# A softmax attention kernel: its row sums spread by one selection matmul, and the reciprocal taken of the spread sums

## What is computed

```python
x = x + attention(_ln_c(x))       # 8 heads of 16 channels
t = x.reshape(768, 128)
t = t + ffn(_ln_t(t))
# attention, per head:
att = q @ k.T / sqrt(16) + time_bias + particle_bias, masked by time
att = softmax(att, axis=-1)
y   = concat over heads(att @ v) @ Wo
# ffn: 8 experts (128 -> 512 -> 128), all of them, for each of the 2 gate weights of a token
h   = gelu((x * p_i) @ W1 + b1);  out += h @ W2 + sum(b2)
```

## Time and profile before

| | |
|---|---|
| median of 3 runs | 2684.5 us |
| the profiled execution, its own time | 2693.18 us |
| its span, first to last instruction | 2691.2 us |
| mean granted TensorE clock, share of full speed | 0.897 |
| PE matmul busy | 2328.3 us (87%) |
| DVE busy | 1373.4 us (51%) |
| ACT busy | 1661.6 us (62%) |
| POOL busy | 1050.5 us (39%) |

### The profile page before, as it was taken

The page is one execution under the profiler, slowest core; times in us unless marked ns, Lnnn a source line. Parts: engine busy times, 40 slices in busy tenths (PEclk is TensorE's granted clock), DMA queues, the critical chain, the costliest instruction groups (busy, mean ns, idle before and its releaser), DMA issues.

```text
span 2691.2 us, 54396 instructions
## 1 busy us (share of the span) xinstructions
PE 2328.3 (87%) x17443; PEld 2071.1 (77%) x17443; DVE 1373.4 (51%) x3267; ACT 1661.6 (62%) x2760; POOL 1050.5 (39%) x1048
## 2 busy tenths in 40 slices
PE   1659988898898989988898998989889898998889
PEld 0448887787878878887787888778787887888778
DVE  2324473554537544573554547455463654447354
ACT  3227567566665657666566765757666566756757
POOL 1104343343434434352443434434342443434347
PEclk7668898999989989998999899989998998899899
DMA  3413022030212203022130302203021120302200
GB/s 47 75 38 45 8 30 26 14 45 7 34 19 33 26 9 47 10 27 26 21 38 7 42 11 32 27 10 45 10 28 26 28 30 8 49 7 30 26 10 7
DMA packets 70219, 71.22 MB, mean 26 GB/s; under 512 B 20462, under 2 KB 55242, under 8 KB 69962
## 3 DMA queue, kind: packets, MB, share of 16 engines
q1 hardware_dynamic: 69746, 67.64, 18.3%
q10 hardware_dynamic: 216, 0.08, 0.0%
HBM read 11.22 MB, written 6.29 MB: 7 GB/s over the span
## 4 chain that ended last, share of the span: by engine, by line
PE 64%; issue 12%; DVE 11%; ACT 9%; SPq 2%; POOL 1%; DMA 0%; DVEq 0%; ACTq 0%; POOLq 0%
PE acc L858 18%; PE wide L784 9%; PE narrow L798 7%; PE zps L847 7%; PE zps L848 5%; PE zps L849 5%; ACT z L490 5%; PE wide L769 5%; DVE maxes L633 3%; DVE h L691 2%; PE wide L812 2%; PE wide L819 2%; PE wide L805 1%; ACT L490 1%; ACT h L519 1%
## 5 line engine op out<-in xcount | busy, mean ns | idle before, releaser
L431 POOL TENSOR_TENSOR hsum<-h 128x384 f32<-128x384 f32 x1024 | 1028.8, 1008 | 1553.6 <-ACT h L519 1533.3
L691 DVE TENSOR_TENSOR h<-zps,ratio_b 128x384 f32<-128x384 f32 x1024 | 561.0, 552 | 928.2 <-PE zps L849 925.9
L518 ACT ACTIVATE h<-zps,b_col 128x384 f32<-128x384 f32 x1024 | 593.5, 580 | 678.4 <-DVE h L691 659.2
L858 PE MATMUL acc<-w,hsum 128*128 128x128 f32 x6144 | 872.3, 279 | 1.5 <-DVE outt L700 1.2
L858 PEld LDWEIGHTS acc<-w,hsum 128*128 128x128 f32 x6144 | 857.1, 196 | 2.2 <-POOL hsum L431 1.7
L519 ACT ACTIVATE h<-h,b_col 128x384 f32<-128x384 f32 x1024 | 620.5, 606 | 0.0
L847 PE MATMUL zps<-x_hi,w_lo 128*128 128x384 f32 x1024 | 428.6, 419 | 88.2 <-DVE x_lo L670 47.9
L633 DVE TENSOR_REDUCE maxes<-wide 128x1 f32<-128x128 f32 (+5 forms) x768 | 437.3, 616 | 87.5 <-PE wide L769 83.8
L784 PE MATMUL wide<-stack 128*128 128x256 f32 (+3 forms) x1280 | 348.9, 432 | 108.2 <-ACT z L490 82.9
L784 PEld LDWEIGHTS wide<-stack 128*128 128x128 f32 x1280 | 264.1, 284 | 187.4 <-ACT z L490 159.0
L490 ACT ACTIVATE z<-wide 128x896 f32<-128x896 f32 (+2 forms) x384 | 343.5, 916 | 63.8 <-PE wide L784 54.9
(11 more groups left out here) (89 smaller groups left out, 1282.8 us busy)
## 6 DMA issues: line engine op xcount, KB each, us to landing
stack<-halves SPq DMA_DIRECT2D x384, 96.0 KB, 3.0
stack<-halves SPq DMA_DIRECT2D x384, 24.0 KB, 2.6
x_in<-in_x SPq DMA_DIRECT2D x136, 48.0 KB, 2.4
out_dram<-outt SPq DMA_DIRECT2D x256, 24.0 KB, 1.6
w<-in_L_ffn_W SPq DMA_DIRECT2D x8, 256.0 KB, 4.3
stack<-max_rows SPq DMA_DIRECT2D x128, 3.0 KB
stack<-max_rows SPq DMA_DIRECT2D x128, 1.5 KB
stack<-z SPq DMA_DIRECT2D x6, 192.0 KB
```

The costliest lines, as they stand in the source:

```text
L431: pool.tensor_tensor(hsum[:, m % NHS, :], h0[:, m % 2, :], h1[:, m % NH1, :], ALU.add).then_inc(hsum_ready, 1)
L518: act.activation(h0[:, m % 2, :], zps[m % 2][:, 0:CT], ACT.Gelu, bias=b1_col[:, j:j + 1]).then_inc(h0_ready, 1)
L691: vec.tensor_tensor(h1[:, m % NH1, :], zps[m % 2][:, 0:CT], ratio_b[:, c * CT:(c + 1) * CT], ALU.mult).then_inc(z1_ready, 1)
L858: ins = pe.matmul(acc[:, n * P:(n + 1) * P], hsum[:, k % NHS, n * P:(n + 1) * P], w2[:, j, :], start=(j == 0 and n == 0), stop=(j == UNITS ...
```

## The change

- Steps *sums* are gone, with `recip` and its small reciprocal.
- `pick` becomes a 128x128 matrix: column c of head hh's 32 columns has a one in row 32hh+16, so it selects that head's sum. In *divide* it is the weights, and `mixed` streams through it in two matmuls of 512 and 256 columns. That gives, in one step, each head's sum repeated over its 32 rows, 128x768.
- DVE then takes the reciprocal of all 128x768 in place in PSUM, waits for its own result (`inverted`), and multiplies `mixed` with it.
- *divide* of group 0 moves to slot 31, ahead of the two *maxima* there; *divide* of group 1 to slot 46, and *project* from slot 49 to 48.
- `xn_ready` after the gate's scaling counts once per half, so the first *split* waits for three of the six products instead of all.

```diff
--- before.py
+++ after.py
@@ -63,10 +63,10 @@
     for hh in range(GH):
         plan += [(26, "scores", (0, hh, n)) for n in range(3)] + [(26, "stack", (1, hh))]
     plan += [(27, "mix", (0, 0)), (28, "mix", (0, 1))]
-    late = [(30, "sums", 0), (32, "divide", 0)] + maxima(1, (31, 31, 32, 33, 34, 36, 36, 37, 38, 39, 39, 40))
+    late = [(31, "divide", 0)] + maxima(1, (31, 31, 32, 33, 34, 36, 36, 37, 38, 39, 39, 40))
     plan += sorted(late, key=lambda step: step[0]) + [(41, "rows", 1)]
     plan += [(44, "scores", (1, n // 3, n % 3)) for n in range(12)]
-    plan += [(44, "mix", (1, 0)), (45, "mix", (1, 1)), (46, "sums", 1), (47, "divide", 1), (49, "project", 0), (50, "load", 1)]
+    plan += [(44, "mix", (1, 0)), (45, "mix", (1, 1)), (46, "divide", 1), (48, "project", 0), (50, "load", 1)]
     plan += [(50, "stats", 1), (51, "seed", 1), (51, "root", (1, 0)), (52, "root", (1, 1)), (52, "root", (1, 2)),
              (54, "scale", (1, 0)), (54, "scale", (1, 1)), (56, "turn", 1), (57, "gate", 0), (58, "weigh", 0),
              (60, "split", 0), (60, "split", 1)]
@@ -74,7 +74,7 @@
 
 
 PLAN = attention_plan()
-WIDE_STEPS = ("turn", "query", "key", "value", "maxima", "rows", "scores", "sums", "divide", "project", "split")
+WIDE_STEPS = ("turn", "query", "key", "value", "maxima", "rows", "scores", "divide", "project", "split")
 NARROW_STEPS = ("mix", "gate")
 
 WIDE = {(s, a): n for n, (s, a) in enumerate([(s, a) for _, s, a in PLAN if s in WIDE_STEPS])}
@@ -128,7 +128,7 @@
         wo_pad = sb("wo_pad", [P, GROUPS, C])
         wg = sb("wg", [P, EXPERTS])
         ident = sb("ident", [P, P])
-        pick = sb("pick", [P, GH])
+        pick = sb("pick", [P, GH, 2 * HD])
 
 
         x_in = sb("x_in", [P, TILES, C])
@@ -145,7 +145,6 @@
         kst = stack[:, HEADS * QW:].rearrange("p (h t) -> p h t", h=GH)
         z = sb("z", [P, GH, ZW])
         maxes = sb("maxes", [P, GH * TILES])
-        recip = sb("recip", [P, TILES, GH])
         max_rows = sb("max_rows", [GH * TILES, P])
         stats = act_t[:, 0:TILES * 6].rearrange("p (i s) -> p i s", s=6)
         moments = sb("moments", [P, TILES, 2])
@@ -228,6 +227,7 @@
         gate_exped = sem("gate_exped")
         split_high = sem("split_high")
         res_ready = sem("res_ready")
+        inverted = sem("inverted")
 
         z_filled = sem("z_filled")
         z1_ready = sem("z1_ready")
@@ -387,7 +387,7 @@
 
         @block.gpsimd
         def _(pool):
-            cleared = ((wo_pad[:, :, :], 0.0), (ident[:, :], 0.0), (hot_stage, 0.0), (pick[:, :], 0.0),
+            cleared = ((wo_pad[:, :, :], 0.0), (ident[:, :], 0.0), (hot_stage, 0.0), (pick[:, :, :], 0.0),
                        (twos, 2.0), (ones, 1.0), (t_hl, 0.0), (p_hl, 0.0))
             later = ((kst[32:64, :, :].bitcast(F32), 0.0), (kst[64:P, :, :].bitcast(F32), 0.0),
                      (spread[0:40, :, 0:PAD], 0.0), (val[:, :, :, HD:2 * HD], 1.0))
@@ -400,7 +400,7 @@
                 done += 1
 
 
-            hots = [(ident[:, :], 0, [[-1, P]]), (pick[:, :], -HD, [[-32, GH]])]
+            hots = [(ident[:, :], 0, [[-1, P]]), (pick[:, :, :].rearrange("p a b -> p (a b)"), -HD, [[-32, GH], [0, 2 * HD]])]
             times, parts = [[-1, TPT], [0, PARTS]], [[0, TPT], [-1, PARTS]]
             hots += [(hot_stage[0:TPT, :], 0, times), (hot_stage[32:32 + PART_N, :], 1, parts)]
             for buf, base, pattern in hots:
@@ -632,15 +632,14 @@
                     for i, at in (((0, 0), (5, P)), ((4, P), (1, 6 * P)), ((3, P), (2, 5 * P)))[part]:
                         ins = vec.tensor_reduce(maxes[:, hh * TILES + i:hh * TILES + i + 1], w[:, at:at + (i + 1) * P], AX.X, ALU.max)
                     ins.then_inc(wide_free[s], 1)
-                elif step == "sums":
-                    vec.wait_ge(wide_filled[s], filled)
-                    vec.reciprocal(recip[:, :, :], w[:, 0:TILES * GH].rearrange("p (i g) -> p i g", g=GH)).then_inc(wide_free[s], 1)
                 elif step == "divide":
                     vec.wait_ge(wide_filled[s], filled)
                     if a == 1:
 
                         for hh in range(GH):
                             vec.wait_ge(stack_loaded[hh], r.at(GROUPS * STACK_DMAS * 16, GROUPS * STACK_DMAS * 16))
+                    vec.reciprocal(w[:, 0:TOK], w[:, 0:TOK]).then_inc(inverted, 1)
+                    vec.wait_ge(inverted, r.at(GROUPS, a + 1))
                     vec.tensor_tensor(mixed_n[a][:, 0:TOK], mixed[:, :], w[:, 0:TOK], ALU.mult).then_inc(wide_free[s], 1)
                 elif step == "project":
                     vec.wait_ge(wide_filled[s], filled)
@@ -663,7 +662,8 @@
                     vec.tensor_tensor(ratio[:, :, 1], top[:, :, 1], gate_r[:, :], ALU.mult)
                     for i in range(TILES):
                         ins = vec.tensor_scalar(xn[:, i, :], xn[:, i, :], top[:, i, 0:1], None, ALU.mult)
-                    ins.then_inc(xn_ready, 1)
+                        if i % HT == HT - 1:
+                            ins.then_inc(xn_ready, 1)
                     assert chain[0] == VCHAIN
                 elif step == "split":
                     vec.wait_ge(split_high, r.at(4, 2 * a + 2))
@@ -742,7 +742,7 @@
                     if not (isinstance(free, int) and free <= 0):
                         pe.wait_ge(narrow_free, free)
                 if step == "turn":
-                    pe.wait_ge(xn_ready, r.at(5, 2 * (a + 1)))
+                    pe.wait_ge(xn_ready, r.at(6, 2 * (a + 1)))
                     for i in range(TILES):
                         ins = pe.transpose(w[:, i * P:(i + 1) * P], xn[:, i, :], ident[:, :])
                     ins.then_inc(wide_filled[s], 1)
@@ -798,20 +798,12 @@
                             ins = pe.matmul(narrow[32 * hh:32 * hh + 32, q0:width], val[:, i, g * GH + hh, :],
                                             z[:, hh, at:at + width - q0], start=(n == 0), stop=(n == len(tiles) - 1))
                     ins.then_inc(narrow_filled, 1)
-                elif step == "sums":
+                elif step == "divide":
 
                     pe.wait_ge(narrow_free, r.at(NPB, NARROW["mix", (a, 1)] + 1))
-                    for i in range(TILES):
-                        ins = pe.matmul(w[:, i * GH:(i + 1) * GH], mixed[:, i * P:(i + 1) * P], pick[:, :], start=True, stop=True)
-                    ins.then_inc(wide_filled[s], 1)
-                elif step == "divide":
-
-                    pe.wait_ge(*taken(r, "sums", a))
-                    for i in range(TILES):
-                        for hh in range(GH):
-                            ins = pe.matmul(w[32 * hh:32 * hh + 32, i * P:(i + 1) * P], recip[:, i, hh:hh + 1].broadcast_to([P, 32]),
-                                            ident[:, :], start=True, stop=True)
-                    ins.then_inc(wide_filled[s], 1)
+                    sums = pick[:, :, :].rearrange("p h d -> p (h d)")
+                    pe.matmul(w[:, 0:QCOLS], sums, mixed[:, 0:QCOLS], start=True, stop=True)
+                    pe.matmul(w[:, QCOLS:TOK], sums, mixed[:, QCOLS:TOK], start=True, stop=True).then_inc(wide_filled[s], 1)
                 elif step == "project":
                     pe.wait_ge(*taken(r, "divide", 1))
                     for i in range(TILES):
@@ -826,7 +818,7 @@
                                         start=True, stop=True)
                     ins.then_inc(narrow_filled, 1)
                 elif step == "split":
-                    pe.wait_ge(xn_ready, r.at(5, 5))
+                    pe.wait_ge(xn_ready, r.at(6, 5 + a))
                     for n in range(HT):
                         i = a * HT + n
                         pe.transpose(w[:, n * P:(n + 1) * P], xn[:, i, :], ident[:, :])
```

## The result

| | before | after |
|---|---|---|
| median | 2684.86 us (4 runs, 2684.5 to 2685.81) | 2854.35 us (4 runs, 2849.92 to 2858.97) |
| the profiled execution, own time | 2693.18 us | 2858.61 us |
| its span | 2691.2 us | 2856.8 us |
| mean granted TensorE clock | 0.897 | 0.870 |

The ratio is 1.0631, with a 95% interval of 1.0608 to 1.0654: slower by 169.5 us. The forecast was 141 us more, 2826 us, with a range of 2770 to 2880. The direction and the mechanism held; the size was 28 us short. It lies 4 us above the 2800 to 2850 that stood for the forecast case (chance 0.63), towards the case with the clock low for twice as long (0.05).

A forecast was written before the change was run, and what follows sets the result against it. It took PE as the bound (busy 87%), with DVE also full around group 0's division. Per round 4.45 + 1.0 + 2.1 + 1.45 = 9.0 us, times 15 = 135, plus 6.3 before the loop: +141, 2826 us, range 2770 to 2880.

The forecast's parts named there:

- the forecast case: Whole kernel: clock loss behind the PE waits within a few tenths of the forecast, 2800 to 2850 us, chance 0.63.
- the case with the clock low for twice as long: Behind both PE waits: a larger loss, bounded at 2.9 us each, chance 0.05.
- The reciprocal's duration: DVE in both divisions: 768 elements at 6.4 ns each plus 153 ns fixed take 5.1 us.
- Rival C: DVE in both divisions: slower reciprocal, 8.3 ns an element, 6.55 us, giving 2872 us; chance 0.09.
- E: DVE rival: part of the small reciprocals' difference is the source, 3.2 ns an element, 2.6 us, about 2703 us; chance 0.03.
- Rival D: DVE: cheap reciprocal, nearly all fixed cost, 0.95 us for 768 elements, so faster, 2660 us; chance 0.03.
- The net -1.65 us of PE per group: PE in each division: 2.94 us of sums and divide go, two selection matmuls of 1.29 us come in.
- Group 0's wait and its carry-over: Slot 31: PE stands 5.7 us for DVE before the second maxima step, and DVE ends up 4.45 us later.
- Group 1's wait and carry-over: Before the projection: PE stands 3.8 us for DVE, and the next unit starts 2.1 us later.
- The clock: Behind both PE waits the clock falls to 0.50: +1.0 us in group 0, +1.45 in group 1, bounds 0 and 2.9 each.
- Given back: Rest of the round: other edits costed at nothing, though the earlier split could give up to 5 us in all.
- In front of the loop: Attention before the loop: two divisions, each 3.15 us longer with no units to hide it, together +6.3 us.

The follow-up runs named there:

- kernel 7: Kernel before with only group 0 changed to selection matmuls and a reciprocal deferred to slot 44, group 1 as before: 2684.98 us, 0.9992.
- kernel 4: Changed kernel with matmuls nobody reads put into PE's two waits, 8 before the second maxima step and 6 before the projection: 2825.08 us, 1.0509 to the kernel before.
- kernel 5: Kernel before with the count of xn_ready per half as the only edit: 2686.77 us, 0.9993.
- kernel 9: Kernel before with the projection in slot 48 instead of 49 as the only edit: 2686.23 us, 0.9999.
- kernel 10: Kernel before with five matmuls nobody reads put into PE's wait between the split and unit 64: 2686.01 us, 0.9997.
- kernel 1: Changed kernel with a copy of the same 128x768 in place of the reciprocal in both groups: 2663.01 us, 0.9912 to the kernel before.
- kernel 3: Changed kernel with a copy in place of the reciprocal in group 1 alone: 2742.38 us, 1.0210 to the kernel before.
- kernel 6: Changed kernel with group 0's reciprocal moved to slot 44 and group 1's split in two, the first beside the second mix: 2637.77 us, 0.9816 to the kernel before.
- kernel 8: Kernel before with group 1 selected and inverted in two pieces, projection in slot 48, xn_ready per half, group 0 as before: 2651.86 us, 0.9871.

## Why the prediction was right, and where its size was off

- **The reciprocal's duration** (5.1 us): 4.97 measured. The slope, 6.4 ns an element from two small rows, measures 6.25. Rival C's rate of 8.3 and E's of 3.2 are both ruled out, and so is D's.
- **The net -1.65 us of PE per group:** the selection's matmuls are spaced as forecast, but where the saving lands matters more. In group 0 only 0.70 us of it shows even when the reciprocal is out of the way (kernel 7), so PE's matmuls were not the only limit there. The sum for the changed kernel had this right, since it went by DVE in group 0.
- **Group 0's wait and its carry-over** (5.7 and +4.45 us): the wait was 5.59. With the clock held up the stage is 36.19 - 31.30 = 4.89 us longer, against 4.45.
- **Group 1's wait and carry-over** (3.8 and +2.1): the wait was 4.01. With the clock held up, 33.64 - 30.52 = 3.12, 1.0 more than forecast. Of this, 0.6 lies in front of the division: from group 1's first mix matmul to the next unit kernel 4 takes 4.35 us and the kernel before 3.74, with the clock low for 3.0 us of it instead of 1.8. The other 0.4 I cannot assign.
- **The clock** (1.0 and 1.45): this is the term that was too small. Kernel 4 gives 1.60 in group 0 and 2.15 in group 1 (of which 2.44 in the projection, less 0.3 elsewhere in the stage). I took the 1.44 us of one short idle stretch as the price of any; behind the longer waits the clock stayed down for 3 us in some rounds and for 6 in others, and through the whole projection in all of them. I had that as the bound (2.9) and not as the value.
- **Given back:** I had costed the rest of the round at nothing. Behind the gate the changed kernel is 1.51 us a round faster than before. In the kernel before, the clock falls there behind two waits of PE in each round; in most rounds of the changed kernel the query comes 3.1 instead of 4.7 us after turn 0, at full speed. All kernels with group 1's new form but kernel 4 have it. In the kernel before, neither the `xn_ready` edit (kernel 5) nor the projection's slot (kernel 9, 0.64 of it at most) nor work put into PE's wait behind the split (kernel 10) brings it.
- **What the rounds show of it:** the query comes 4.7 us after turn 0 in all 14 rounds of the kernel before, and 3.1 in 11 of the changed kernel's; in the other three it takes 4.5, 5.8 and 5.8, and the two 5.8 are the rounds of 174.0 us. It takes 3.1 in every round of kernels 1, 3 and 6. In kernel 8 the rounds in which the clock falls there are 2.5 to 3.0 us longer than the others; in kernel 9 some 0.5, and there the rounds without that fall have the clock low for twice as long behind the split. Kernel 4 is not a clean case: in 6 of its 14 rounds the clock is at 1.00 from turn 0 to the query, and it still takes 4.2 to 4.8 us. PE stands there (1.29 us in one of them) for something that the profile does not show.
- **What that leaves open:** the rounds of the kernel before and of kernels 5, 7, 9 and 10 all average 160.40 to 160.45 us, though a stage of kernels 7, 9 and 10 is 0.5 to 0.7 us shorter; what one stage gains, others lose. So four times "no change" does not show that these edits are worth nothing where the rounds are not held at that length, and none of them was taken out of the changed kernel by itself. What decides where the clock falls, and what holds the rounds at 160.4, is not shown.
- **In front of the loop** (+6.3): DVE takes up the first projected batch at 178.8 us instead of 172.2, 6.6 later. That agreement is in part luck. In kernels 5, 9 and 10 this comes at 168.6, 166.3 and 165.5 with the same work in front of it as in the kernel before, so one trace each cannot measure a difference of 6 us.
- **The sum:** 1.0 and 1.7 a round too little in the groups, 1.5 too little given back, with 0.5 in the rest; 1.7 x 15 = 26 us, less some 1 outside the loop, which is the 25 by which the profiled span (+165.6) exceeds the 141. (The medians lie 169.5 apart, since the profiled execution was 8.3 us above its median before and 4.3 after.) That the time fell inside the range is in part luck: without the 1.5 given back it would be some 23 us more by this table, an estimate of 2877, at the very end of the range (2880).
- **Rival D** gave 2660 for a cheap reciprocal, and kernel 1 measured 2663.01. That agreement is luck: D had 1.65 us a round from group 1, where kernel 1 gives 0.94, loses 0.72 in group 0, and owes its gain to the 1.76 behind the gate, which the rival's working did not hold. That the change pays with an operation of 0.97 us in place of the reciprocal is shown by kernel 1; at which duration the sign turns was not measured.

One thing stays unexplained beside the mean: the four runs of the changed kernel lie at 2850 (twice) and 2859 (twice). The four of the kernel before spread over 1.3 us, but its 23 beside kernels 8 to 10 over 9 (2683.89 to 2692.75). The rounds of the changed kernel take 170.1 to 174.0 us, those of the kernel before 160.3 to 160.7; two rounds of 174.0 stand in the profiled execution.

## What to carry to other kernels

An operation that is cheap on 24 elements is not cheap on 768: take its duration an element from two small rows of it, and look at which queue it stands in, since everything behind it in program order waits too. Here the fewer matmuls were a gain only once the same 5 us of reciprocal stood where DVE was idle or PE not yet waiting, and no PSUM tile that PE wants next hung on them: 2637.77 us against 2854.35 with the same arithmetic. Against the kernel before, the two places where the edits are gave only 1.36 of the 3.44 us a round; most of the rest came behind the gate, for a reason not shown. So compare stages, and single rounds, before you credit a gain to an edit. And a wait put into PE's stream costs the wait plus what it does to the clock behind it, which should be bounded by the longest low stretch seen, not by one short example; removing a low stretch at one place can bring it back at the next wait.

## What the runs showed of the hardware

- DVE's reciprocal, float32, 128 partitions: 4.966 us for 768 elements from PSUM in place, 4.942 from SBUF, 3.358 for 512 and 1.758 for 256 (PSUM to SBUF):

```profile
L649 DVE RECIPROCAL act_t<-act_t 128x768 f32<-128x768 f32 x16 | 79.1, 4942 | 0.0
L644 DVE RECIPROCAL halves<-wide 128x512 f32<-128x512 f32 x16 | 53.7, 3358 | 35.4 <-PE wide L813 35.4
L644 DVE RECIPROCAL halves<-wide 128x256 f32<-128x256 f32 x16 | 28.1, 1758 | 4.9 <-PE wide L813 4.9
```

  The slope between 256 and 512 is 1600 / 256 = 6.25 ns an element, six times the 1.04 ns of a simple operation, and 158 ns are fixed. In place in PSUM it takes 24 ns more on 768 elements than in place in SBUF. For results written to SBUF, the Trainium skill (VectorE: DVE Perf Modes, section on the TRN2 errata) gives 62 cycles more from PSUM than from SBUF; 554 and 553 ns for 384 elements do not bear that out.
- The granted clock after the same wait of 5.59 us at the same place of a round was back at 1.00 after some 3 us in six of 15 rounds and after 6 in nine.
- With PE kept at work in a wait the clock stayed at 1.00 behind it each time, and in kernel 10 the mean clock was 0.910 against 0.901 without a change in the time.
- With the clock low behind turn 0, that step and the two units behind it took 1.6 us more (4.7 against 3.1) in both kernels 8 and 9; the rounds were 2.5 to 3.0 us longer in kernel 8 and some 0.5 in kernel 9. The PE waits ahead of it were nearly the same (2.75 and 2.45 us in the two rounds of kernel 8 shown).
